# Graph attention kernel on one core: front, row boundary, tail and preparation reordered, and x and the first weights requested only when two planes are zeroed

## The reference

```python
h = jnp.maximum(_layernorm(x, axis=-1), 0.0)
x = x + _L0_gnn_ref(h, adj, rel_pair_index, Wq, bq, Wk, bk)
h = jnp.maximum(_layernorm(x, axis=-1), 0.0)
x = x + _L1_gnn_ref(h, adj, W_seq, a1, a2, W_out, b_out)
```

```python
scores = scores.at[:, sub, obj].set(att)          # att = q[sub] . k[obj] / 8
scores = jnp.where(mask[None], -jnp.inf, scores)
scores = scores.at[:, di, di].set(1e-07)
attn = jax.nn.softmax(scores, axis=2)
return (attn.sum(axis=0) / HEADS) @ inst_feature
```

## Time and profile before

| | us |
|---|---|
| median of 3 runs (lowest, highest) | 1249.17 (1247.87, 1250.72) |
| the profiled execution's own time | 1243.49 |
| its span, first to last instruction | 1241.8 |
| PE busy | 1111.4 (90%) |
| DVE busy | 958.5 (77%) |
| ACT busy | 810.8 (65%) |
| POOL busy | 124.3 (10%) |

### The profile page before, as it was taken

How to read it: one execution, slowest core, us unless ns; L and a number is a source line. 1 busy time by engine, 2 the same in 40 slices (tenths; PEclk the granted TensorE clock), 3 DMA queues, 4 the chain that set the end, 5 groups by cost and what they waited for, 6 DMA issues and landing times. The chain is left out here.

```text
span 1241.8 us, 24778 instructions
## 1 busy us (share of the span) xinstructions
PE 1111.4 (90%) x10557; PEld 766.2 (62%) x10562; DVE 958.5 (77%) x1319; ACT 810.8 (65%) x843; POOL 124.3 (10%) x143
## 2 busy tenths in 40 slices
PE   4799696999999999999885599999999999999697
PEld 3344242444444444444342599999999999999443
DVE  2380326999999999998821799999999999998265
ACT  1321536667667776675512899999999999996022
POOL 3678630000000000000000000000000000000011
PEclk9899897999999999999898699999999999999799
DMA  9530270322222121000430111110011001100422
GB/s 352 104 23 1 70 154 31 79 46 62 62 62 57 42 43 45 26 35 25 161 119 13 69 36 37 44 62 36 36 36 36 37 36 36 36 36 3 160 78 77
DMA packets 35213, 77.69 MB, mean 63 GB/s; under 512 B 5669, under 2 KB 10658, under 8 KB 33058
## 3 DMA queue, kind: packets, MB, share of 16 engines
q1 hardware_dynamic: 27314, 60.55, 13.9%
q0 software_dynamic: 7792, 15.58, 7.0%
HBM read 65.39 MB, written 23.21 MB: 71 GB/s over the span
## 5 line engine op out<-in xcount | busy, mean ns | idle before, releaser
L1250 ACT ACTIVATE area_h<-area_a,s 128x2048 fp8e4<-128x2048 f32 x208 | 396.7, 1988 | 0.5 <-DMA area_a<-s_rows 0.5
L1402 PE MATMUL psum<-s_V,area_h 128*128 128x198 bf16 x2048 | 286.7, 249 | 0.0
L1403 PE MATMUL psum<-s_V,nadjT 128*128 128x99 bf16 x2048 | 280.7, 209 | 0.0
L1399 PE MATMUL psum<-s_V,area_h 128*128 128x99 bf16 x2048 | 206.0, 210 | 20.2 <-DVE area_b L1303 19.6
L1400 PE MATMUL psum<-s_V,area_b 128*128 128x99 bf16 x2048 | 205.9, 209 | 0.0
L1399 PEld LDWEIGHTS psum<-s_V,area_h 128*128 128x128 fp8e4 x2048 | 189.7, 98 | 20.8 <-issue 20.6
L1402 PEld LDWEIGHTS psum<-s_V,area_h 128*128 128x128 fp8e4 x2048 | 199.9, 98 | 0.2
L1403 PEld LDWEIGHTS psum<-s_V,nadjT 128*128 128x128 fp8e4 x2048 | 199.8, 98 | 0.0
L1400 PEld LDWEIGHTS psum<-s_V,area_b 128*128 128x128 fp8e4 x2048 | 189.7, 98 | 0.0
L641 PE MATMUL psum<-area_h,s_WT 128*128 128x512 f32 x384 | 180.8, 598 | 0.9 <-ACT s_WT L765 0.9
L1298 DVE TENSOR_TENSOR area_h<-area_h,area_a 128x512 uint32<-128x512 uint32 x256 | 171.7, 687 | 12.4 <-ACT area_h L1250 8.0
(11 more groups left out here) (154 smaller groups left out, 1169.2 us busy)
## 6 DMA issues: line engine op xcount, KB each, us to landing
area_a<-s_rows SPq DMA_DIRECT2D x16, 1024.0 KB, 4.7
rel_planes<-s_zero POOLq DMA_DIRECT2D x3, 2304.0 KB, 23.7
f_late<-rel_planes SPq DMA_DIRECT2D x36, 192.0 KB, 3.0
area_h<-in_x SPq DMA_DIRECT2D x4, 1024.0 KB, 20.3
f_adj<-in_adj POOLq DMA_DIRECT2D x16, 256.0 KB, 6.8
s_x<-in_x SPq DMA_DIRECT2D x16, 256.0 KB, 2.5
adj_chunks<-s_chunk SPq DMA_DIRECT2D x16, 256.0 KB, 2.1
x<-s_x SPq DMA_DIRECT2D x16, 256.0 KB, 2.0
```

Source lines behind the costliest of these rows:

```text
L1250: act.activation(masks[:, j, :], s1b[:, b, :], ACT.Relu, bias=t["s2"][:, n, 0, j:j + 1], scale=BIG, saturate=False).then_inc(signs, 1)
L1399: pe.matmul(out[:, :, 0:DZ], masks[:, j, cols], V[:, b, j, :, 0:DZ], **first)
L1402: pe.matmul(out, masks[:, j, cols], V[:, b, j, :, :], **first)
L1403: last = pe.matmul(out[:, :, DZ:CZ], nadjT[:, NEAR_TILES.index(j), cols], V[:, b, j, :, DZ:CZ], **then)
```

## The change

What it does, by place:

- **Opening.** SyncE waits until the second plane is zeroed before it requests x and the weights. The number of scatters in stage 1 is 56.
- **Stage 1.** The counts and own edges of the unrelated tiles, their factor chain, the turn and copy of chunk 0 and the sixth load of `adj` are moved in from stage 2. ScalarE's first exponentials are there too.
- **Front of stage 2.** Gathering stands first; chunks NU + 1 and 3 are turned beside gather 2, NU + 2 behind it; the first scores stand behind the gathers; heads 2 to 7 of row 0 are scored one by one (`score_head`); the low tile of row 0 is made after the copies of NU + 2. Loads of `adj` from the eighth on wait for the first related row.
- **Row boundary.** On VectorE `finish` and `clear` stand ahead of `factors`, and `measure` ahead of `add_diagonal`; scores, masks, exponentials and sums run over 1500 columns instead of 1536.
- **Tail.** The last four steps are written out: turns stand ahead of the products of the block before, row 11 starts with blocks 6 and 7, and sums in bank 0. The inversion of `adj` and the standard deviation are moved in from stage 3.
- **Preparation (stage 3).** The maximum goes over TensorE; the sign is multiplied in stage 4.
- **Stage 4 and 5.** ScalarE's first two packs stand behind signs 0 and 1; W_out and its bias are requested in stage 4.

The core of the diff (repeated or plain moves left out):

```diff
-FIRST_SCATTERS = 60
+FIRST_SCATTERS = 56
...
             sp.dma_start(rel[0:EP, :, :], io["L0_gnn_rel_pair_index"]...).then_inc(rel_in, 16)
+            sp.wait_ge(f.plane_zero[1], 16)
             load_x(0)
             load_w(K, "L0_gnn_Wk")
...
             f.scatter(pool, t, 8 + 4 * ADJ_RING, FIRST_SCATTERS)
+            pool.wait_ge(f.chunk0_ready, 4)
+            pool.wait_ge(own_ready, 1)
+            f.load_adj(pool, io, ADJ_RING)
...
-            biased(8, G)
+            biased(8, 12)
...
+            for u in range(NU):
+                biased(12 + 2 * u, 14 + 2 * u)
+
+                act.wait_ge(f.adj_in[u], 16)
+                if u:
+                    act.wait_ge(counted, u)
+                act.activation(f.chunk0[:, :, :].rearrange("p j i -> p (j i)"), f.adjn[:, u, :], ACT.Copy, saturate=False,
+                               accum_out=f.nu[:, u:u + 1]).then_inc(counted, 1)
+            act.wait_ge(counted, NU)
+            for q in range(4):
+                act.wait_ge(adj_turned, q + 1)
...
+            biased(20, G)
...
-            project(12, G, 20)
+            project(12, 20, 20)
+            pe.wait_ge(f.adj_in[0], 16)
+            for j in range(NT):
+                last = pe.matmul(ps[:, j // 4, j % 4 * P:(j % 4 + 1) * P], f.adjn[:, 0, j * P:(j + 1) * P], t["identb"][:, :],
+                                 start=True, stop=True)
...
+            project(20, G, 20)
...
+            f.scatter(pool, t, FIRST_SCATTERS, FIRST_SCATTERS + 12)
+            load_adj(NU + 2)
+            f.scatter(pool, t, FIRST_SCATTERS + 12, EC)
+            pool.wait_ge(f.rel_in[0], 16 * PLANES)
+            for k in range(NU + 3, NT):
+                load_adj(k)
...
+            def score_head(r, hd):
+
+                pe.wait_ge(masked, HA * r + hd - 1)
+                for ch in range(CH):
+                    last = score_chunk(r, hd // 2, hd % 2, ch)
+                last.then_inc(scores, 1)
...
                 copy_one_and_scores(-1)
+                relu(1)
+                copy_h(1)
+                for q in range(4):
+                    copy_adj(NU + 2, q)
+                f.make_low(act, 0)
                 count(0)
...
+            def last_steps():
+                r = ET - 2
+                turn_w(r, 0)
+                project(ET)
+                aggregate(r, 0)
+                turn_one_and_scores(ET - 1)
+                for m in range(2, 7):
+                    turn_w(r, m)
+                    aggregate(r, m - 1)
+                turn_h(ET + 1)
+                aggregate(r, 6)
+                turn_w(r, 7)
+                project(ET + 1)
+                aggregate(r, 7)
+                turn_one_and_scores(ET)
+                r = ET - 1
+                turn_w(r, 6)
+                turn_w(r, 7)
+                aggregate(r, 6)
+                turn_w(r, 0)
+                aggregate(r, 7)
...
-            pool.wait_ge(topped, 1)
-            pool.partition_all_reduce(topa[:, :], top[:, :], P, bass.bass_isa.ReduceOp.max).then_inc(top_all, 1)
+            pool.memset(ones[:, :], 1.0).then_inc(consts, 1)
...
+            load(1, 1)
+            sp.dma_start(t["wout"][:, :, :], io["L1_gnn_W_out"].rearrange("(t p) n -> p t n", p=P)).then_inc(t["wout_in"], 16)
...
+                    if n == 0 and j in (0, 1):
+                        pack(0, 0, j)
                     if j in (9, 14) and n < HB - 1:
                         pack(n + 1, 1 - b, 0 if j == 9 else 1)
-            pack(0, 0, 0)
-            pack(0, 0, 1)
```

More of the change, by code:

```diff
@@ L175, in make_low @@
         act.wait_ge(self.marked, it + 1)
-        act.activation(self.low[it % 2], self.scored, ACT.Identity, bias=self.minus_big[:, 0:1],
+        act.activation(self.low[it % 2][:, 0:NREL], self.scored[:, 0:NREL], ACT.Identity, bias=self.minus_big[:, 0:1],
                        scale=BIG).then_inc(self.low_ready, 1)
@@ L408, in stage2 @@
     WT = [sb(f"WT{i}", [P, 2, P]) for i in range(2)]
-    chunk = [sb(f"chunk{i}", [P, NT, P], F8) for i in range(3)]
+    chunk = [f.chunk0] + [sb(f"chunk{i}", [P, NT, P], F8) for i in (1, 2)]
     xt = [sb(f"x{i}", [P, D]) for i in range(3)]
@@ L461, in rank, with turned_round @@
         return RANK.get(k, k)
+    def turned_round(r, m):
+        return no["one", r + 1] if m == 1 and r < ET - 1 else no["w", r, m]
     with nc.Block() as block:
@@ L566, in begin_round, with score_chunk @@
                 count[0] += 1
+            def score_chunk(r, p, half, ch):
+                rows, cols = slice(half * DK, (half + 1) * DK), slice(ch * 512, min(NREL, (ch + 1) * 512))
+                return pe.matmul(ps[:, 3 * half + ch, 0:cols.stop - cols.start], qk[rows, Q, p, r * P:(r + 1) * P],
+                                 qk[rows, K, p, cols], start=True, stop=True)
             def score(r, p):
@@ L666, in front @@
             def front():
-                score(0, 0)
-                for q in range(4):
-                    turn_adj(0, q)
                 for i in range(8):
@@ L1581, in build @@
         with ExitStack() as first:
-            f = FirstLayer(nc, first, area_a, area_b)
+            f = FirstLayer(nc, first, area_a, area_b, late)
             with ExitStack() as part:
```

420 lines of the change are left out of this document (227 added, 193 removed).

## The result

| | before | after |
|---|---|---|
| median, us (lowest to highest) | 1248.52 (1247.61 to 1250.72) | 1215.72 (1213.73 to 1218.34) |
| ratio, 95% interval | | 0.9736 (0.9709 to 0.9763) |
| the profiled execution's own time | 1243.49 | 1217.59 |

The change makes the kernel 2.6% faster, 32.8 us. The forecast was 1229.5, 19.7 less, with a range of 1215 to 1241: the time lies 0.7 us inside its lower end, and three fifths of the gain were foreseen. A second comparison on another chip gave 0.9754 (0.9728 to 0.978).

What follows compares the result with a forecast made beforehand. TensorE and VectorE were taken as near their limit in the first attention and TensorE in stage 4, so gains lie in the seams; 1.9 - 4.7 - 3.9 - 5.2 - 5.4 + 2.0 - 4.4 = -19.7, so 1229.5 us, range 1215 to 1241.

Steps and rivals of the forecast that it cites:

- Opening: Stage 1: holding x and Wk until planes 0 and 1 are zero costs +1.9 us, bounds -5 and +29.
- I take 8.3 us as its start: Start of stage 1: the software queue with the planes begins at 8.3 us, so x is released at 21.5 to 22.
- Rival C: Start of stage 1: the software queue starts when issued, x is 7 us earlier, 1223 us; chance 0.10 together with another rival.
- Front: Start of stage 2: first mask 56.1 us after its opening, first factors 23.6 later; -4.7 us, bounds -8 and 0.
- Steps: Twelve rows of the first attention: 0.35 us less a step from fewer columns, eleven steps -3.9, bounds -1 and -9.
- rival B: Attention steps: VectorE's ring sets them, a step would be 32.9 us, -29 instead of -3.9, giving 1204; chance 0.08.
- TensorE from the turn of row r to the fourth score: Attention steps: this stretch, then one mask, an exponential and the copy of h, closes the ring; 0.35 us less a step.
- Tail: End of the first attention: reordered turns and products end TensorE at +61.9 instead of +67.1; -5.2 us, bounds -7 and -3.
- Stage 3: Preparation: root's turnaround, wait for GpSimd's maximum, inversions and sign product go, about 1.5 us is new; -5.4, bounds -6.5, -3.5.
- stage 4: Its start: packs stand behind signs 0 and 1, each later sign is 2.1 us late; +2.0, bounds +0.9, +2.2.
- Stage 5: Its start: output weights already there, no 4.3 us wait for the bias; -4.4 us, bounds -6.5, -2.
- A removed microsecond is the same in both: Whole kernel: differences summed against the profile may be set on the median, 5.7 us above it.

## Why the prediction was right in sign and two fifths short

The time fell inside the range by 0.7 us, and that is luck in part: six of the seven terms were off to the same side (stage 4 alone by 0.3 to the other), and one, the tail, lies outside its own bounds. Below, the forecast of each term stands against the lower pair of profiles where no pair is named.

**Opening: the sign was wrong (+1.9, measured -1.4).** The step that failed is "I take 8.3 us as its start". I read GpSimd's silence until 8 us as a start-up cost; it was the bytes of x and the weights on SyncE's queue, which the hold removes. Rival C had this half right: the planes start when issued, and x is released at 16.7. The other half of C was too large, since the third plane then takes the DMA engines, and the first projections come 2.5 us before my 39.7, not 7. The second group comes 2.8 early, and the 16 turns of chunk 0 take 0.89 and not 1.8: together the 3.6 by which TensorE ends ahead of my 134.3. The Trainium skill ("DMA: Bandwidth & Descriptors", Anatomy of one DMA), which I set aside because of the start, was nearer: an estimate by its figures puts the release near 15, and the trace has it at 16.7. What my sum lacked altogether is the end of the stage: I had GpSimd "done near 118", by its instructions, and did not ask when its last DMA lands. With the hold this did no harm, since TensorE ends last; without it the landing sets the opening. The hold bought nothing by itself: 56 scatters with it and without it end the stage at the same time, with TensorE last in the one case and the load in the other (131.7 and 132.0).

**Front: -4.7 against -4.8 in the first pair of profiles, and -5.8 to -6.7 in the paired ones; the match is luck.** The first mask came to the tenth. From there to the first factors I had 23.6 (its parts add up to 23.4), with the six single heads one after the other at 2.6 each and one stretch at half clock. The second profile of the changed kernel has that one stretch and takes 21.9:

```profile
189.61 6.60 PE L630 MATMUL psum<-area_a 64*128 64x512 f32 x12 [3.99 <-DVE s_negm L1120]
196.80 4.42 PE L630 MATMUL psum<-area_a 64*128 64x512 f32 x12 [0.58 <-DVE s_negm L1120]
201.40 4.42 PE L630 MATMUL psum<-area_a 64*128 64x512 f32 x12 [0.18 <-DVE s_negm L1120]
```

Each row is two single heads. They overlap: two take 4.42 us and not 5.2, since the second starts 1.64 after the first, when VectorE's next mask is done, and not when the first has ended (2.78). The first profile has a second stretch at half clock, loses the 1.5 us again, and so meets my number.

**Steps: the size within bounds, the reason half right.** I forecast intervals of 35.1 to 35.2; the steady ones are 35.22. That the columns alone bring this is confirmed by the runs with the old order and with 1536 columns, and rival B is refuted: no steady interval came near 32.9, and VectorE's order was worth nothing. But "TensorE from the turn of row r to the fourth score" is wrong behind the second score, where VectorE's seven us a pair set the pace as well. Seven steady intervals make 2.1 us; the rest of the term (-5.4 to -6.5 in all) lies in the two first and two last intervals, above all in the last: 36.6 in the kernel before, with scores at half clock, 34.5 now. In the run with 1536 columns it is 36.6 again, and in the run without the hold, with 1500, it is 36.2: whether these scores fall to half clock is not decided by the columns alone.

**Tail: -5.2, measured -7.4 and -9.0, outside the bounds of -7 and -3.** The order gave about 6.1 in both pairs: without the stretches at half clock the tail is 62.8 before and 56.7 after, in all four profiles. The rest is projections at half clock (normal is 3.70). The kernel before, first profile, has one of 6.65 and its second profile two, of 6.59 and 5.40:

```profile
608.46 6.65 PE L663 MATMUL psum<-s_wseq,s_h2T 128*128 128x512 f32 x8 [1.68 <-ACT s_WT L765]
```

The changed kernel has one of 5.40 in each, the last of the tail in its first profile and the first in its second:

```profile
599.69 3.70 PE L737 MATMUL psum<-s_wseq,s_h2T 128*128 128x512 f32 x8 [1.65 <-ACT s_WT L863]
...
651.57 5.40 PE L737 MATMUL psum<-s_wseq,s_h2T 128*128 128x512 f32 x8 [0.56 <-ACT scores L870]
```

```profile
593.80 5.40 PE L737 MATMUL psum<-s_wseq,s_h2T 128*128 128x512 f32 x8 [1.65 <-ACT s_WT L863]
```

I walked the new order with "the durations of before", and so carried the 6.65 over.

**Stage 3 (-5.4 against -5.5 to -6.2), stage 4 (+2.0 against +1.8 to +2.3): right.** Putting the packs first gives most of it back, so it was the order of the packs.

**Stage 5: -4.4 against -4.9 to -6.0.** I took out the 4.3 of waiting and left the first projection nearly at half clock; it takes 4.62 to 4.87 and not 6.10. The run with the late weights brings 5.5 back.

**The baseline.** "A removed microsecond is the same in both" failed: the 5.7 us between profile and median are not an offset that every execution carries but half-clock stretches in some of them, and they change with the kernel. In all, of the 12 us by which the sum fell short of the lower pair, 3.3 are the opening, 2.0 the front, 2.6 the steps, 2.2 the tail and 1.6 stage 5 (stage 3 and 4 make up the rest); apart from the opening about half of them are places where TensorE runs at 2.4 GHz now and ran at 1.2 before (the last interval of the steps 1.7, the tail 1.25, the projection of stage 5 1.5); the others are above all the overlap of the single heads and an order of the tail that gave 0.9 more than I had walked. I had priced each wait at its length and not at what follows it.

## What to carry to other kernels

Count a wait of TensorE not by its length alone but look at the durations behind it: in the last step of the kernel before a wait of 2.14 us was followed by scores of 4.49 us, and with the wait at 1.71 they took 2.79. Then take more than one profile, since the same wait was also seen with either duration behind it. Ask of every stage that ends with all engines meeting when its last DMA lands, not when it is requested: a load moved ahead of the last requests, with two scatters moved out, opened the next stage 6 us sooner, where holding x back gave none. And before you order an engine's instructions anew to fill its waits, find which stretch of the ring it sets: the same 1.7 us was worth 1.3 in one half of the step and 0.5 in the other.

## What the runs showed of the hardware

- The end of a stage came after the landing of GpSimd's last DMA: a load of 256 KB requested at 124.26 moved bytes until 129 and landed near 130, and the next stage opened at 132.0, 6.3 us after TensorE was done. With the load requested at 115.24 and the last scatter at 121.14 it opened at 126.0, 1.3 us after TensorE.
- DMA requests that GpSimd issued at 1.7 us moved bytes from 3 us on when SyncE had only a small load out, and only after 8 us when SyncE requested x and the weights from 1.4 us on (GpSimd's queue moved 0.41 MB at 4 to 5 us in the one case and none in the other). SyncE's queue moved 1.35 MB at 2 to 8 us, more than its request for 1 MB of x at 1.35 us and the small load ahead of it, so requests that SyncE issued later (from 1.81 us on) held back an earlier one of GpSimd.
- After a wait of the same length the granted clock of TensorE was at either level: 1.82 us in both profiles of the changed kernel, then 1.2 GHz (5.37 us) in one and 2.4 GHz (2.79) in the other. With 1.72 us of TensorE's work less in each step, three intervals of eleven grew by 1.6 us and nothing was left of the gain, in the one execution that there is.
- Scores of single heads on the two halves of the array's rows overlapped although each was issued by itself: two that started 1.64 us apart took 4.42 us, each of them 2.78, which is what a pair issued side by side takes (2.79).
